# Count matrix of a graph network: a tile takes two turns at least instead of three, one ring of mark buffers, tiles written out, degrees read back in a later phase

## The reference

```
for _ in range(NUM_STEPS):                      # 6
    h = jnp.maximum(node_feats @ W1.T + b1, 0.0) @ W2.T + b2
    msg = jax.ops.segment_sum(h[src], dst, num_segments=n_nodes)
    gx = msg @ W_ih.T + b_ih
    gh = node_feats @ W_hh.T + b_hh
    ...                                         # gates, new node_feats
...
x = x + gnn(layernorm(x), src, dst) + linear_attention(layernorm(x))
```

## Time and profile before

| | us |
|---|---|
| median of three runs | 4173.86 |
| the profiled execution, its own time | 4137.55 |
| its span | 4135.8 |
| setup, and the start of adjacency up to the first product | 45.6 |
| adjacency, first product to last product | 320.7 |
| from there to the next phase's first instruction | 16.9 |
| addition phase "mix" | 9.2 |
| gated graph and all later phases | the rest |

### The profile page before, as it was taken

The page is one execution under the profiler, slowest core; times in us unless marked ns, Lnnn a source line. Parts: engine busy times, 40 slices in busy tenths (PEclk is TensorE's granted clock), DMA queues, the critical chain, the costliest instruction groups (busy, mean ns, idle before and its releaser), DMA issues. The chain is left out here.

```text
span 4135.8 us, 62159 instructions
## 1 busy us (share of the span) xinstructions
PE 3729.9 (90%) x19129; PEld 3108.8 (75%) x19130; DVE 2572.8 (62%) x5167; ACT 1520.3 (37%) x3547; POOL 756.2 (18%) x613
## 2 busy tenths in 40 slices
PE   5885869999999999999997699877999999879995
PEld 2553448989989899898896588744888888758884
DVE  7776675555555655655655555544777777577774
ACT  0354212121121211211211444333888886135552
POOL 0000000000000000000000300002888886012221
PEclk9998989999999999999998899988999999779997
DMA  1242112222222222222220211011333332411113
GB/s 41 62 86 57 71 42 77 85 73 83 86 68 87 69 81 88 67 86 84 72 86 31 69 32 31 16 35 53 93 94 94 94 93 71 168 48 37 36 35 111
DMA packets 297720, 288.61 MB, mean 70 GB/s; under 512 B 101483, under 2 KB 272846, under 8 KB 296805
## 3 DMA queue, kind: packets, MB, share of 16 engines
q1 hardware_dynamic: 233867, 208.55, 16.7%
q0 software_dynamic: 56576, 66.41, 6.1%
q10 hardware_dynamic: 7002, 10.15, 0.7%
HBM read 241.89 MB, written 42.72 MB: 69 GB/s over the span
## 5 line engine op out<-in xcount | busy, mean ns | idle before, releaser
L946 PE MATMUL bank<-a_wide,parts 125*128 125x448 f32 x4200 | 873.8, 367 | 0.0
L946 PEld LDWEIGHTS bank<-a_wide,parts 125*128 125x128 f32 x4200 | 785.9, 188 | 79.1 <-issue 9.9
L2080 POOL DMA_INDIRECT rows<-h_dram,src_t x400 | 494.4, 1236 | 123.2 <-DVE prod L2269 86.1
L2196 ACT ACTIVATE hot<-eq,ea 125x80 f32<-125x80 f32 x1600 | 413.3, 351 | 0.0
L906 POOL TENSOR_TENSOR nf_g<-nf,nf_g 128x896 fp32r<-128x896 f32 x42 | 94.5, 2250 | 1626.1 <-ACT nf_g L1106 1626.1
L1014 DVE CAST a_wide<-a_cols 125x2240 fp32r<-125x2240 bf16 x210 | 274.2, 1322 | 142.3 <-PE bank L946 142.0
L955 PE MATMUL bank<-nf_g,whh 128*128 128x448 f32 x1512 | 339.1, 369 | 0.0
L955 PE MATMUL bank<-msg,wc 128*128 128x448 f32 x1512 | 338.4, 368 | 0.0
L2122 PEld LDWEIGHTS bank<-prod,hot 125*80 125x80 f32 x2400 | 295.0, 150 | 54.0 <-issue 0.7
L2122 PE MATMUL bank<-prod,hot 125*80 125x128 f32 x2400 | 328.4, 273 | 0.0
L955 PEld LDWEIGHTS bank<-msg,wc 128*128 128x128 f32 x1512 | 284.3, 188 | 26.7
(11 more groups left out here) (419 smaller groups left out, 5957.7 us busy)
## 6 DMA issues: line engine op xcount, KB each, us to landing
a_cols<-a_dram SPq DMA_DIRECT2D x210, 546.9 KB
a_dram<-a_cols SPq DMA_DIRECT2D x16, 1250.0 KB, 8.0
w<-in_w SPq DMA_DIRECT2D x4, 2728.0 KB
deg_bc<-deg_dram SPq DMA_DIRECT2D x42, 224.0 KB, 5.8
gate_bc<-gate_dram SPq DMA_DIRECT2D x42, 224.0 KB, 3.2
rows<-h_dram,src_t POOLq DMA_INDIRECT x400, 4.1
y<-y_rows SPq DMA_DIRECT2D x12, 512.0 KB, 10.9
w<-in_w SPq DMA_DIRECT2D x5, 1024.0 KB
```

The source lines that it names most:

```text
L946: ins = nc.tensor.matmul(p_msg[f][:, 0:GW], parts[0:SPB, m, c * HB + k, f * 128:(f + 1) * 128], a_wide[u % 2][0:SPB, k, :], start=(c == 0 ...
L2080: nc.gpsimd.indirect_dma_start(out=rows[n % ITC][:, :], out_offset=None, in_=h_dram, in_offset=bass.IndirectOffsetOnAxis(ap=src_t[:, n:n + ...
L2196: ins = nc.scalar.activation(hot[:, q % 2, j, m, :], eq[:, q % 2, j, :], ACT.Copy, scale=ea4[:, q * UC + j, m:m + 1])
```

## The change

It does four things.

- `SPAN` is 4 instead of 6: a tile takes two turns at least. `NDT` is 79 instead of 80 (the tile that holds only padding is gone), so A in DRAM has rows of 3160 instead of 3200 columns. `setup` stores a third number for each tile, its count of turns.
- One ring `hot` of four buffers (`SLOTS` = 4) for every turn, picked by the register `turns`. On DVE all turns of a tile are in the register loop; on PE the first turn stands ahead of the loop and the others are in it.
- The outer loop is gone: 79 tiles are written out on each engine. The addresses of `fetch` are then fixed numbers. ACT waits on the count of turns that PE has done, and loads the tile's own count from `ranges` for it. Stores are of five tiles each (15 of them), then of three and of one.
- The end of the phase (the read-back, the sums, the test, the degrees' store) moves into a new phase `add_mix_and_degrees`, which takes the place of `add_transposed("mix")`: the transposes use five banks, and the small operations stand between fixed tiles of the 25.

```diff
-NDT = NP // DW
-TT = NDT // NM // 2
-TC = TT * DW
+NDT = -(-N // DW)
+SETS = [5] * 15 + [3, 1]
-SPAN = 6
+SPAN = 4
-SLOTS = 2
+SLOTS = 4
...
-            phase(adjacency, sems, sb, bank, hots, a_dram, deg_dram, crowded_t)
+            phase(adjacency, sems, sb, bank, hots, a_dram)
...
-                phase(add_transposed, "mix", sems, bank, sb, ident, x_rows, mix)
+                phase(add_mix_and_degrees, sems, bank, sb, ident, x_rows, mix, a_dram, deg_dram, crowded_t)
...
-                then(nc.vector.tensor_scalar(even[:, :], even[:, :], -2, None, ALU.bitwise_and))
-                then(nc.vector.tensor_copy(last[:, :], even[:, :]))
-                nc.vector.tensor_tensor(range_i[:, 1:2], first[:, :], last[:, :], ALU.add).then_inc(tiles_done, 1)
+                then(nc.vector.tensor_scalar(range_i[:, 2:3], even[:, :], 1, None, ALU.arith_shift_right))
+                then(nc.vector.tensor_copy(last[:, :], range_i[:, 2:3]))
+                nc.vector.tensor_copy(range_i[:, 0:1], first[:, :]).then_inc(tiles_done, 1)
+                nc.vector.scalar_tensor_tensor(out=range_i[:, 1:2], in0=last[:, :], scalar=2.0, in1=first[:, :],
+                                               op0=ALU.mult, op1=ALU.add).then_inc(tiles_done, 2)
...
+                eng.reg_load(at[t % 2][k], ranges[0:1, t, k:k + 1])
...
+        def turn_slot(eng, turns):
             v = eng.snap(turns, min_val=0, max_val=NDT * NCH)
+            return v, hot[:, bass.ds(v & (SLOTS - 1), 1), :, :].rearrange("p o c w -> p (o c) w")
...
+                for n, (t, tiles) in enumerate(zip(firsts, SETS)):
+                    sp.wait_ge(cols_done, START + (t + tiles) * HALVES)
+                    sp.dma_start(a_dram[:, :, t * DW:(t + tiles) * DW], a_cols[n % 2][:, :, 0:tiles * DW]).then_inc(stored[n % 2], 16)
...
+                for t in range(NDT):
+                    first, past = tile_range(dve, at, t)
+                    fetch(dve, at, t + 1)
+                    dve.wait_ge(rel_done, START + t + 1)
+                    with dve.Fori(first, past, 2) as u:
+                        v, slot = turn_slot(dve, turns)
+                        dve.wait_ge(turn_used, START + v - (SLOTS - 1))
+                        for c in range(2):
+                            ins = nc.vector.tensor_scalar(slot[:, c, :], iota_at[:, :], edge_rel[:, t % RELS, bass.ds(u + c, 1)],
+                                                          None, ALU.is_equal)
+                        ins.then_inc(turn_done, 1)
+                        dve.reg_add(turns, turns, 1)
...
+                def turn(to, u, begins):
+
+                    v, slot = turn_slot(pe, turns)
+                    pe.wait_ge(turn_done, START + v + 1)
                     for c in range(2):
                         lo = hot_lo[:, :, bass.ds(u + c, 1)].rearrange("p w o -> p (w o)")
                         for h in range(HALVES):
+                            ins = nc.tensor.matmul(to[h], lo, slot[:, c, h * HW:(h + 1) * HW], start=begins and c == 0, stop=False,
+                                                   skip_group_check=True)
+                    ins.then_inc(turn_used, 1)
+                    pe.reg_add(turns, turns, 1)
+                for t in range(NDT):
+                    first, past = tile_range(pe, at, t)
+                    to = [bank[(t % 2) * HALVES + h][:, 0:HW] for h in range(HALVES)]
+                    pe.wait_ge(cols_done, START + (t - 1) * HALVES)
+                    turn(to, first, True)
+                    fetch(pe, at, t + 1)
+                    with pe.Fori(first + 2, past, 2) as u:
+                        turn(to, u, False)
...
+                    for t in range(start, start + tiles):
+                        act.reg_load(rounds, ranges[0:1, t, 2:3])
+                        act.reg_add(turns, turns, rounds)
+                        act.wait_ge(turn_used, START + act.snap(turns, min_val=2, max_val=NDT * NCH))
...
+def add_mix_and_degrees(nc, sems, bank, sb, ident, x_rows, mix, a_dram, deg_dram, crowded_t):
...
+        p_t, p_deg, p_bad = bank[0:5], bank[5:7], bank[7]
...
+                for t in range(NT):
+                    pe.wait_ge(added, START + t - 4)
+                    for k in range(KD):
+                        ins = nc.tensor.transpose(p_t[t % 5][0:RT, k * 128:(k + 1) * 128], mix[:, k, t * RT:(t + 1) * RT], ident[:, :])
+                    ins.then_inc(turned, 1)
+                    if t == 15:
+                        pe.wait_ge(cut_done, START + 1)
+                        pe.wait_ge(rows_in, START + 16)
+                        for n in range(2):
+                            nc.tensor.matmul(p_deg[n][0:CUTS, 0:half], cut_sum[:, :], by_cut[:, n * half:(n + 1) * half],
+                                             start=True, stop=True).then_inc(deg_mm, 1)
```

More of the change, by code:

```diff
@@ L664, in _, with adjacency @@
                                                  bias=bo[:, f:f + 1], scale=1.0).then_inc(mix_done, 1)
[L667 to L672, removed]
+def adjacency(nc, sems, sb, bank, hots, a_dram):
+    rel_done, turn_done, turn_used, cols_done, stored_0, stored_1 = sems(*("a_" + s for s in (
+        "rel turn_done turn_used cols stored_0 stored_1").split()))
     stored = (stored_0, stored_1)
@@ L786, in turn @@
                         for h in range(HALVES):
-                            ins = nc.tensor.matmul(to[h], lo, slot[:, c, h * HW:(h + 1) * HW], start=start and c == 0,
-                                                   stop=stop and c == 1, skip_group_check=True)
-                    return ins
-                with pe.Fori(0, NM) as g:
-                    for j in range(2 * TT):
-                        t = g * (2 * TT) + j
-                        first, past = tile_range(pe, at, j)
-                        to = [bank[(j % 2) * HALVES + h][:, 0:HW] for h in range(HALVES)]
-                        pe.wait_ge(cols_done, START + (t - 1) * HALVES)
-                        pe.wait_ge(first_done, START + t + 1)
-                        turn(to, hot_first[:, j % 2, :, :], first, True, False).then_inc(first_used, 1)
-                        fetch(pe, at, j + 1, t + 1)
-                        with pe.Fori(first + 2, past - 2, 2) as u:
-                            v, slot = mid_slot(pe, turns)
-                            pe.wait_ge(mid_done, START + v + 1)
-                            turn(to, slot, u, False, False).then_inc(mid_used, 1)
-                            pe.reg_add(turns, turns, 1)
-                        pe.wait_ge(last_done, START + t + 1)
-                        turn(to, hot_last[:, j % 2, :, :], past - 2, False, True).then_inc(acc_mm, 1)
@@ L806, in _ @@
-                pe.wait_ge(cols_done, START + NDT * HALVES)
-                pe.wait_ge(cut_done, START + 1)
-                pe.wait_ge(rows_in, START + 16)
-                for n in range(2):
-                    nc.tensor.matmul(p_deg[n][0:CUTS, 0:half], cut_sum[:, :], by_cut[:, n * half:(n + 1) * half], start=True, stop=True)\
-                      .then_inc(deg_mm, 1)
-                pe.wait_ge(bad_done, START + 2)
-                nc.tensor.matmul(p_bad[0:1, 0:1], bad[:, :], ones[0:KT * CUTS, :], start=True, stop=True).then_inc(bad_mm, 1)
+                            ins = nc.tensor.matmul(to[h], lo, slot[:, c, h * HW:(h + 1) * HW], start=begins and c == 0, stop=False,
+                                                   skip_group_check=True)
@@ L815, in _, with relative @@
             @block.scalar
             def _(act):
-                def relative(t, b):
-                    nc.scalar.activation(edge_rel[:, b, :], edge_at[:, :], ACT.Identity, bias=tile_at[:, bass.ds(t, 1)], scale=1.0)\
+                turns, rounds = (act.alloc_register(f"a_{n}_act") for n in ("turns", "rounds"))
+                act.reg_mov(turns, 0)
+                def relative(t):
+                    nc.scalar.activation(edge_rel[:, t % RELS, :], edge_at[:, :], ACT.Identity, bias=tile_at[:, t:t + 1], scale=1.0)\
@@ L820, in relative @@
                       .then_inc(rel_done, 1)
                 for t in range(RELS):
[L822 to L829 removed]
+                    relative(t)
```

172 lines of the change are left out of this document (80 added, 92 removed).

## The result

The changed kernel takes 4218.78 us (median of 4 runs, 4214.75 to 4224.36), the kernel before 4172.89 beside it (median of 4): a ratio of 1.0111, 95% interval 1.0093 to 1.0128. That is 45.9 us more, where 30.2 were forecast (4204 us, range 4176 to 4232). The profiled execution took 4214.75 us, its span is 4213.1.

The account below looks back on a forecast made before the run. PE's sequencer, by its register work, was taken to bound adjacency's small tiles. Adjacency +32.3, the phase's end -3.7 and the addition phase +1.6 gave +30.2 us on 4173.86: 4204 us, range 4176 to 4232.

Parts of the forecast that it names:

- The tile: Adjacency: a tile of two turns takes 2.77 us of PE's sequencer steps, with bounds 2.65 and 2.90.
- 3.06 us apart in the last 40 tiles: Sign in adjacency's profile: PE's bank waits, one a tile, come 3.06 us apart there, and 4.2 in tiles of three turns.
- DVE, ACT, SP at nothing: Adjacency: the edits on these engines cost nothing; DVE's tile of two turns takes 2.3 to 2.5 us, under PE's 2.77.
- issue over 100, DVE under 15: Sign in adjacency's profile: PE's waits for "issue" grow to over 100 us while those for DVE stay under 15.
- The clock: Adjacency: counted on the full granted clock, 1.00; below 1.00 before the last tile would show the prediction wrong.
- The end of the phase: Adjacency's last product to the next phase: 13.3 us, bounds 10.8 and 15, so 3.7 us less than before.
- Setup at 0: Setup phase: seven tiny steps are swapped for seven, so its time changes by 0.
- gated_graph: Phase gated_graph: shorter rows of A change only where its loads begin; 0 us, bounds -1 and +3.
- Steps hidden: Rival in adjacency: first turn's register steps run under the array, two-turn tile 2.04 us; 4146 us, chance 0.12.
- in between: Rival in adjacency: a tile takes about 2.4 us, so no change; 4174 us, chance 0.08.
- Fetch stalls: Rival in adjacency: fetching written-out tiles, 16 to 24 packets, stalls PE 1.3 us each; +21 to +31, 4230 us, chance 0.09.
- it doesn't do what it says: Case in adjacency: tiles at the end still meet more than four chunks; excluded for all but five of the last 40.

Follow-up runs that it names:

- run 79: Not a label of one run: the words belong to "Run by run 79 rows", the kernels with setup's arrays on 79 rows; setup ended at 47.5 to 50.8 us.

## Why the prediction was right, and where its terms were off

**What bounds the kernel: right.** PE's sequencer sets the tile in the changed kernel, and did in the small tiles before; in the long loops before, two buffers passed between DVE and PE, as the prediction had it. Every load that was added counted in full, half the columns counted nothing, the same products went into 1.80 us for two turns once there were fewer steps, and one turn with a fixed address was worth 0.49 us.

**The tile: 2.77 us predicted, 2.82 measured.** The 0.05 is the bank's wait: before, it and the range step had 0.15 together; after, each is a step of 0.10. This was between my value and the bound of 2.90. It makes 79 x 0.05 = 4 us. The repeated turn is 1.14 (1.13) at first reading. Slow loads cost 17.6 us in all (by summing what each load took above 0.30), 0.22 a tile, for my 0.29; that gives back 5.5 us. In smooth stretches they come in one tile of five, the one beside a store, both loads of it:

```profile
L691 PEldq TENSOR_LOAD <-ranges x2: 927/948/970, 204.7 to 205.7; - x2
```

Sum: 79 x (2.82 + 0.22) + 98 x 1.14 = 352; measured are 357.0, predicted 353.0. So the sum misses 5 us now, where it missed 0.6 before. Of these, 2 are the repeated turn, which is 1.16 in the longer tiles (1.17 three times, 1.13 once), and not 1.14. The other 3.3 are short gaps between PE's steps, 31 of them and each 0.06 to 0.19 us longer than is usual between the same two lines. All 31 lie within 6 us of one of the 11 packets in which instructions were fetched (below, at the rivals). The term was +36.3 for +32.3.

The warning sign "3.06 us apart in the last 40 tiles" read 3.27; five of these tiles have three turns, which makes 0.14 of it.

**DVE, ACT, SP at nothing: right.** DVE waits for PE 93.2 us, and its marks are always early. The warning sign "PE waits for DVE" did show up in the waits, and the sign "issue over 100, DVE under 15" did not, for PE itself (14.8 and 49.2 beside the start). This was a wrong step in reading: with the buffer's wait now ahead of every turn, the profile puts the sequencer's gaps down to DVE. "Issue" shows in PEld's row.

**The clock: nearly.** It was 0.97 in the window and not 1.00. That it falls below 1.00 before the last tile was one of my signs of being wrong. The sign came, but with half the columns at a clock of 0.58 the time was the same, and no run shows a cost of it.

**The end of the phase: 13.3 predicted, 14.2 measured**, -2.7 in place of -3.7, within the bounds of 10.8 and 15. SP issued the last store at 410.7, 1.1 us after the last product, and its issue alone took 1.36. The step that failed is the small store's landing, queued behind its neighbour: it is past 11 us from issue, for my 9.9.

**The addition phase: +1.6 predicted.** From the first addition to the next transfer 12.9 us for 11.6, +1.3; from barrier to barrier +1.5.

**Setup at 0: wrong, and the largest error.** The first product came 7.1 us later. The step said "seven tiny steps for seven" and counted DVE's steps only. It left out that the number of tiles is also the number of partitions that the chunk ends are copied to, and two broadcasts of 80 rows became two of 79. Run by run 79 rows cost 7 to 10 us. The Trainium skill, "DMA: Bandwidth & Descriptors", section "Why a DMA increments its semaphore by 16 and not by 1", says that a transfer is split over the largest number of engines, 16 at most, that divides the slowest dimension of both sides: 16 for 80 rows, one for 79. The traces agree: the packets ran up to 16 at a time with 80 rows and one by one with 79, and the wait grew from 0.6 to 6.9 us.

**n1, +5.3: not foreseen.** The prediction took the phases whose code stays at nothing; it had no term for where a loop comes to lie in the program.

**gated_graph +1.6 in this pair of profiles**, within the bounds of -1 and +3; but a second profile of each has the phase at 1652.8 us before and 1650.1 after, so it is the spread of runs and not the rows of A.

**The rivals.** Steps hidden (4146) and in between (4174): the tile of 2.82 and the added loads exclude both. Fetch stalls (4230): in part. The queue of instructions moved 11 packets for 2 in adjacency:

```profile
q8 instruction: 11, 0.18, 0.2%
```

PE doesn't stall for 1.3 us at each of them, as the rival had it. But tiles of two turns without a slow load, mostly 2.81 to 2.87 apart, come up to 3.05 apart near a packet, and the short gaps named above add 0.3 us a packet. They are there in the same number, 31, and the same 3.3 us in four kernels with these written-out tiles. So writing the tiles out seems to cost 3.3 us and not 21 to 31; that the fetch is the cause is read from the times, no run tested it. The range of packets was also too high, 11 for 16 to 24. The case that it doesn't do what it says: there were 256 turns, as counted.

So the forecast of +30.2 was 15.7 us short of the +45.9: +7.1 for setup, +5.3 for n1, +4.0 for adjacency, +1.0 for the end, less 0.1 for the addition phase make 17.3; the phases without a cause add 0.5, and the medians show 2.1 less than the traces. The time lies within the range of 4176 to 4232, but more than half of what was missing came from two terms, setup and n1, that the prediction had at 0. The 4 us of adjacency are near by some luck: the slow loads were taken 5.5 us too dear, and the longer steps and the gaps were not seen.

## What to carry to other kernels

Where the work of a loop turn is short, count the sequencer's steps of the engine that sets the pace, not the busy time: an address from a register, a register load or a taken branch takes its time as a product does, and removing the turn whose addresses were fixed while making another's variable is a loss. Keep fixed buffers for the turns that every tile has, and put only what varies in number into the loop, with a branch around it. Before changing a count, look for every array and transfer that has this count as a dimension.

## What the runs showed of the hardware

- One row fewer, 79 for 80, held two broadcasts of 125 KB so long that DVE waited 6.9 us in place of 0.6. In the six kernels with 79 rows it waited 6.9 to 10.3 us, and their packets ran one by one; in the seven with 80 rows at most 0.6.
- A loop of 25 short instructions, its code unchanged, took 12.2 us at one place in the program and 17.5 at another. Placing it made it fast again (12.2).
- A register load takes 0.30 us, and 0.91 to 0.99 on PE in the few us behind the issue of a store of A; PE and DVE both have them, mostly once in each set of five tiles.
- On PE a compare-and-branch record lasts 0.21 us when the branch is taken and 0.07 when it falls through (98 and 79 of them in the changed kernel).
- Near each of the 11 instruction packets of adjacency PE's steps have some three gaps that are 0.06 to 0.19 us too long, 0.3 us a packet.
- Register loads into a register that nothing reads do not reach the chip, and two additions that follow loads are one step of 0.10 with the next one.
- The gather of edge_convolution takes 1.24 us on one chip and 1.27 to 1.32 on others, and the whole kernel before 4139 or 4163 to 4173 us; kernels are to be compared on one chip.
